# Cross-attention of a two-layer network: two transposes moved in TensorE's order, one small transfer moved to another queue

## The chip, the core and the metric

The kernel runs on one core of a Trainium2 chip. The metric is the device time of one execution in microseconds (us). Before the change three runs gave 2221.7, 2225.9 and 2228.41 us; the median is 2225.9 us.

TensorE (PE in the profile; PEld is its weight loads) does matrix products and transposes into PSUM, VectorE (DVE) and ScalarE (ACT) work on SBUF and PSUM, GpSimd (POOL) on SBUF, and SyncE (SP) issues most of the DMA transfers. Each engine has its own instruction stream and goes through it in order; the streams are tied together by semaphores.

## The reference

Two layers over 32 batches of 112 tokens with 512 features. The first attends to a context of 375 rows per batch and gates the result. The second does rotary self-attention with two sets of expert weights, then cross-attention over the same context, then a gated MLP with two sets of expert weights. The change lies in the cross-attention of the second layer:

```python
ci = rms_norm(hidden_states, ln_post_cross_w)
cq = heads(ci @ cq_w, NH, CHD)                 # 16 heads of 16
ckv = encoder_outputs @ ckv_w
ck, cv = jnp.split(ckv, 2, axis=-1)
cctx = sdpa(cq, ck, cv, causal=False)          # softmax(cq ck / sqrt(CHD)) cv
hidden_states = hidden_states + cctx.transpose(0, 2, 1, 3).reshape(b, l, CC) @ cdense_w
```

## The kernel before

The kernel runs in stages, each over all batches or token tiles: the first layer (names with `a_`), the projections of the second (`b_`), self-attention (`c_`), its output projection and the queries of the cross-attention (`d_`), the cross-attention (`e_`), and the MLP (`f_`). Products that need full precision are made of three: each operand is split into a high half (rounded to the fp32r type by ScalarE) and a low half (the rest, by VectorE or GpSimd), and `split_products` (lines 109 to 113) multiplies high by high, high by low and low by high.

The cross-attention is a software pipeline. There is one loop over steps `s` in each engine's function (`e_pe`, `e_dve`, `e_act`, `e_sp`, `e_pool`), and a step works on four batches at once: it prepares keys, queries and values of batch `s + 2`, takes the scores and their maxima of batch `s`, computes the scores once more by key with the maxima subtracted, and their exponentials, for batch `s - 1`, and finishes the context and its dense product for batch `s - 2`. The order inside a step is written out by hand for each engine.

TensorE's order in a steady step (`e_pe`, from line 1918): `scores(s, 0)`; `context(s - 2)`; `maximum_turn(s - 1)`, a transpose of the maxima into PSUM bank 7 (line 1890); `scores(s, 1)` (line 1848); `turn(s - 2)`, four transposes of the context (line 1895); `e_key_products(s + 2)`, twelve products into banks 4 and 5; `back(s - 2)`, two transposes of the normalised context (line 1901); `scores(s, 2)`; `queries_turn(s + 2)`, two transposes of the queries into banks 4 and 5 beside the keys (line 1815); `values(s + 2)`, eighteen products into banks 6 and 7; `scores(s, 3)`; `scores_by_key(s - 1, 0)` and `(s - 1, 1)` (line 1867); half of the dense product; and so on to the last groups by key. The scores use banks 0 to 2, and each group waits for the maximum of the group before it. `scores_by_key` writes banks 4 to 7, so its first group waits until the keys and queries of batch `s + 2` have been read from banks 4 and 5 (`e_kq_lo`), and for the transfer of the maxima (`e_max_placed`).

VectorE's order (`e_dve`, from line 2018): `maximum(s, 0)` (line 1970); `maximum_turned(s - 1)`, the copy of the turned maxima to SBUF (line 1987); `maximum(s, 1)`; `norm(s - 2)`, a reciprocal and a product (lines 2003 and 2005), which `back` waits for; `maximum(s, 2)`; `keys_queries_low(s + 2)` (line 1993); the copy of the last values; the low half of the context; the other maxima.

ScalarE's order (`e_act`, from line 1780): `raw(s - 2)`, the copy of the context out of PSUM (line 1769), which `turn` waits for; the high half of the memory (line 1366); the high half of the context, once `back` is done (line 1789); the high half of keys and queries, once the queries are turned (line 1403); values; the exponentials (line 1763); the copy of the dense product.

SyncE's order (`e_sp`, from line 1709): memory and query rows of later batches (lines 1653 and 1658); `place_maximum(s - 1)`, the transfer of the turned maxima, 14 KB, into two rows of the queries' tile (line 1690), which first waits for VectorE's copy; `place_both(s + 1)`, six transfers of keys and six of queries (lines 1675 and 1686); the stores of split keys and queries (line 1661). Behind the stage's loop SyncE loads the first rows of the MLP stage (lines 2079 and 2082), which VectorE adds up (line 2239) and ScalarE squares (line 2149).

Of the kernel before, what the change touches and what calls it, by code (L numbers as in the profile page):

```python
# [5 lines left out]
F32 = mybir.dt.float32  # L6
# [8 lines left out]
BATCHES, SEQ, DIM = 32, 112, 512  # L15
# [6 lines left out]
HEADS, HD = 16, 32  # L22
# [93 lines left out]
def build_xattn(nc, x_t, mem_t, mem_n, mem_e, weights, e_weights, q_weights, w_gate_mem, w_mem, b_gate,  # L116
# [3 lines left out]
    with ExitStack() as ctx:  # L120
# [1241 lines left out]
        def e_memory_high(act, b):  # L1362
            act.wait_ge(e_m_loaded[b % 2], 16 * (b // 2 + 1))
            if b >= 2:
                act.wait_ge(e_v, 2 * (b - 1))
            act.copy(e_m_parts[b % 2][0], e_m[b % 2]).then_inc(e_m_hi, 1)
# [242 lines left out]
        e_max_placed = Later(const_loaded, 16 * len(loads))  # L1609
# [9 lines left out]
        e_queries = [rv(at, (CT, PAIRS, SEQ)) for at in (4096, 5888, 19168)]  # L1619
        e_c_parts = both(20960, (CT, SEQ))  # L1620
        e_max_tok = [rv(25536 + 128 * i, (P,), SEQ) for i in range(2)]
        e_max_t = rv(25792, (SEQ,))
# [4 lines left out]
        def e_split(b):  # L1627

            return b + 2
# [20 lines left out]
        def e_sp(sp):  # L1650
            def load_memory(b):
                sp.wait_ge(e_m_lo, b - 1)
                sp.dma_start(e_m[b % 2], mem_e[b]).then_inc(e_m_loaded[b % 2], 16)

            def load_queries(b):
                if b >= 2:
                    sp.wait_ge(e_k, e_split(b - 2))
                sp.dma_start(e_cq[b % 2], cq_rows[b * SEQ:(b + 1) * SEQ]).then_inc(e_cq_loaded[b % 2], 16)

            def store(b, x, wide, into):  # L1660
                sp.dma_start(into[b, :, x].rearrange("t d (g s) -> (d g) t s", g=PAIRS), e_split_parts(b)[x][:, :, wide].bitcast(F32)).then_inc(
                    e_stored.sem, 16)

            def store_both(b):
                for x, made in enumerate((e_kq_hi, e_kq_lo)):
                    sp.wait_ge(made, e_split(b))
                    store(b, x, keys, k_rows)
                    store(b, x, queries, q_rows)

            def place_keys(b):  # L1670
                sp.wait_ge(*stored(b))
                into, done = e_keys[b % 3].rearrange("p g s -> p (g s)").bitcast(F32), e_placed[b % 2].sem
                for t in range(CT):
                    for part, x in enumerate((0, 1, 0)):
                        sp.dma_start(rows_of(into, t, part), k_rows[b, t, x]).then_inc(done, 16)

            def place_both(b):
                if b < 3:
                    sp.wait_ge(*e_cleared.at(1 if b == 1 else 3))
                else:  # L1680
                    sp.wait_ge(e_st, KEY_UNITS * (b - 2))
                place_keys(b)
                into, done = e_queries[b % 3].rearrange("p t g s -> p t (g s)").bitcast(F32), e_placed[b % 2].sem
                for t in range(CT):
                    for part, x in enumerate((0, 0, 1)):
                        sp.dma_start(rows_of(into, t, part)[:, t], q_rows[b, t, x]).then_inc(done, 16)

            def place_maximum(b):
                sp.wait_ge(e_mxt_made, b + 1)
                sp.dma_start(e_queries[b % 3][MAX_ROW:MAX_ROW + 2].bitcast(F32), e_max_t[0:2 * HEADS].bitcast(F32)).then_inc(  # L1690
                    e_max_placed.sem, 16)

            for b in (2, 3):
                load_memory(b)
            for x, made in enumerate((e_kq_hi, e_kq_lo)):
                sp.wait_ge(made, 1)
                store(0, x, keys, k_rows)
            place_keys(0)
            sp.wait_ge(*d_scattered.at(16 * BLOCKS))
            load_queries(0)  # L1700
            load_queries(1)
            sp.wait_ge(e_ones, 4 + 2 + 1)
            sp.wait_ge(e_kq_hi, 2)
            for part in (0, 1):
                place_queries(sp, part, e_kq_parts[0])
            load_queries(2)
            base = sp.value_load(base_f[0:1, 0:1], min_val=W_F, max_val=W_F + F_CHUNKS)
            store_both(1)
            for s in range(BATCHES + 1):
                if s + 4 < BATCHES:  # L1710
                    load_memory(s + 4)
                if s + 3 < BATCHES:
                    load_queries(s + 3)
                if s:
                    place_maximum(s - 1)
                if s + 1 < BATCHES:
                    place_both(s + 1)
                if s + 2 < BATCHES:
                    store_both(s + 2)
                if 2 <= s < 2 + RING:  # L1720
                    ring_load(sp, M_F + s - 2, chunk_at(base, s - 2))
# [30 lines left out]
        def e_act(act):  # L1752
            def values(b):
                act.wait_ge(e_v, 2 * b + 1)
                act.copy(e_cv[b % 4][:, 0:2, :, 0:CHD], ps[0:KC, e_key_bank(b) + 2, :].rearrange("p (c h d) -> p c h d", c=2, h=HEADS)).then_inc(
                    e_v_act, 1)

            def exponents(b, u):
                act.wait_ge(e_st, KEY_UNITS * b + u + 1)
                if b and u % NKC == 0:  # L1760
                    act.wait_ge(e_ctx, CT * (b - 1) + u // NKC + 1)
                at = 4 + 2 * (u % 2)
                act.activation(e_pt[:, u], ps[0:KC, at:at + 2, 0:4 * SEQ], ACT.Exp).then_inc(e_exp, 1)  # L1763

            def raw(b):
                act.wait_ge(e_ctx, 2 * b + 2)
                if b:
                    act.wait_ge(e_turned, b)
                act.copy(e_raw_t, ps[:, 3, 0:NT]).then_inc(e_raw, 1)

            e_memory_high(act, 2)
            values(0)
            values(1)
            act.wait_ge(e_k, 2)
            e_high(act, 0, queries)
            act.wait_ge(e_kq_lo, 2)
            place_queries(act, 2, e_kq_parts[1])
            act.wait_ge(e_k, e_split(1))
            e_high(act, 1, slice(0, CEVEN + SEQ))
            for s in range(BATCHES + 2):  # L1780
                if s == BATCHES + 1:
                    f_squares(act, 0)
                if s >= 2:
                    raw(s - 2)
                if s + 3 < BATCHES:
                    e_memory_high(act, s + 3)
                if s >= 2:
                    act.wait_ge(e_back, s - 1)
                    act.copy(e_c_parts[0], ps[:, 3, 0:CT * SEQ].rearrange("p (t s) -> p t s", t=CT)).then_inc(e_c_hi, 1)
                if s == BATCHES + 1:  # L1790
                    f_input_high(act, 0)
                if s + 2 < BATCHES:
                    act.wait_ge(e_k, e_split(s + 2))
                    e_high(act, s + 2, slice(0, CEVEN + SEQ))
                    values(s + 2)
                if 4 <= s < 4 + RING:
                    ring_high(act, M_F + s - 4)
                if 1 <= s <= BATCHES:
                    for u in range(KEY_UNITS - 2):
                        exponents(s - 1, u)  # L1800
                if s >= 2:
                    b = s - 2
                    act.wait_ge(e_cd, b + 1)
                    if b >= 2:
                        act.wait_ge(*e_scattered[b % 2].at(16 * (b // 2)))
                    act.copy(e_out[b % 2], ps[0:SEQ, 3, :]).then_inc(e_cd_out, 1)  # L1806
                if 1 <= s <= BATCHES:
                    for u in range(KEY_UNITS - 2, KEY_UNITS):
                        exponents(s - 1, u)

        def e_pe(pe):
# [106 lines left out]
            for s in range(BATCHES + 2):  # L1918
# [3 lines left out]
                if old:  # L1922
                    context(s - 2, 0)
                    context(s - 2, 1)
                if by_key:
                    maximum_turn(s - 1)
                if now:
                    scores(s, 1)
                if old:
                    turn(s - 2)  # L1930
                if new:
# [3 lines left out]
                if s == BATCHES + 1:  # L1935
                    f_turn(pe, 0, 0)
                    f_turn(pe, 0, 1)
                if now:
                    scores(s, 2)
                if new:  # L1940
                    queries_turn(s + 2)
                    values(s + 2, range(NKC))
                if now:
                    scores(s, 3)
# [19 lines left out]
        def e_dve(dve):  # L1964
# [53 lines left out]
            for s in range(BATCHES + 2):  # L2018
                if s < BATCHES:
                    maximum(s, 0)  # L2020
                if 1 <= s <= BATCHES:
                    maximum_turned(s - 1)
                if s < BATCHES:
                    maximum(s, 1)
                if s == BATCHES + 1:
                    f_add(dve, 0)
                    f_means(dve, 0)
# [419 lines left out]
```

## Time and profile before

| | |
|---|---|
| median of three runs | 2225.9 us |
| the profiled execution's own time | 2228.36 us |
| its span, first to last instruction | 2226.6 us |
| mean granted TensorE clock | 0.980 of full speed |
| TensorE busy | 95% of the span |
| VectorE, ScalarE, GpSimd busy | 57%, 47%, 40% |
| cross-attention stage | from about 1001 to 1517 us of the span, 32 steps |

A row of the timeline gives the start in us from the span's start, the length in us, the engine, the line of the kernel, the operation, output and inputs with their shapes, and how many like instructions in a row it merges. In brackets stands the engine's idle time ahead of it and what ended it. Matmuls overlap, so the distance between two starts says more than the length of one.

### The profile page before, as it was taken

Reading aid. Unit: us, or ns where it says so; the run is one execution under the profiler, and the core shown is the slowest. Engines: PE = TensorE matmul, PEld = TensorE weight load, DVE = VectorE, ACT = ScalarE, POOL = GpSimd, SP = SyncE. Lnnn points to the kernel's source line nnn. Section 1 sums busy time; section 2 is a strip of 40 time slices with the busy share of each in tenths; the row PEclk is TensorE's granted clock in tenths of the full one; section 3 lists DMA queues with packets and bytes.
Section 4 is the critical chain, followed back from the end, with each engine's and each line's share of the span. In section 5 each row is a group of like instructions: output and inputs, shape, how many; then the busy total and the mean of one; then the engine's idle time right before and its main releaser. Section 6 shows DMA issues by size and latency. Waiting matters only on the chain.

```text
span 2226.6 us, 40571 instructions
## 1 busy us (share of the span) xinstructions
PE 2117.5 (95%) x16042; PEld 1825.1 (82%) x16042; DVE 1276.0 (57%) x1910; ACT 1055.6 (47%) x1875; POOL 880.1 (40%) x741
## 2 busy tenths in 40 slices
PE   7999999999889889997999999988999999999998
PEld 6899998888667768887888888877888888888887
DVE  6755547756599984545666666654444344444343
ACT  5344335344278765443565555544334334344333
POOL 2211027676534324452111111104454554555456
PEclk9999999999999999997999999989999999999999
DMA  6343335665554446556777777645343443434333
GB/s 238 129 141 127 125 144 178 214 238 203 197 183 144 141 150 244 224 187 186 233 232 211 218 214 206 205 128 191 119 134 117 136 152 109 140 120 129 113 93 121
DMA packets 155613, 373.70 MB, mean 168 GB/s; under 512 B 40160, under 2 KB 60992, under 8 KB 145696
## 3 DMA queue, kind: packets, MB, share of 16 engines
q1 hardware_dynamic: 136416, 310.70, 44.1%
q0 software_dynamic: 18720, 60.29, 7.5%
q8 instruction: 128, 2.10, 0.4%
q14 instruction: 61, 0.50, 0.1%
q10 hardware_dynamic: 288, 0.11, 0.0%
HBM read 269.28 MB, written 100.93 MB: 166 GB/s over the span
## 4 chain that ended last, share of the span: by engine, by line
PE 82%; DVE 12%; DMA 3%; ACT 1%; issue 1%; SPq 0%; POOL 0%; POOLq 0%; DVEq 0%; ACTq 0%
PE ps L111 21%; PE ps L113 21%; PE ps L112 21%; PE ps L1848 5%; PE ps L1880 3%; PE ps L1867 3%; DVE f_arena L1311 2%; DVE c_max L1306 2%; PE ps L688 2%; DVE e_negmax L1970 2%; DVE c_sum L1317 1%; DMA f_arena<-qk_rows 1%; DVE r_arena L179 1%; DVE f_arena L1328 1%; PE ps L1895 1%
## 5 line engine op out<-in xcount | busy, mean ns | idle before, releaser
L111 PE MATMUL ps<-r_arena 128*128 128x512 f32 (+6 forms) x2410 | 894.0, 371 | 17.5 <-DVE r_arena L179 11.1
L112 PE MATMUL ps<-r_arena 128*128 128x512 f32 (+6 forms) x2410 | 882.9, 366 | 0.0
L113 PE MATMUL ps<-r_arena 128*128 128x512 f32 (+6 forms) x2410 | 882.9, 366 | 0.0
L179 POOL TENSOR_TENSOR r_arena<-f_arena,r_arena 128x512 fp32r<-128x512 f32 (+1 forms) x434 | 579.5, 1360 | 571.6 <-ACT r_arena L201 423.2
L111 PEld LDWEIGHTS ps<-r_arena 128*128 128x128 f32 (+2 forms) x2410 | 455.8, 189 | 81.7 <-POOL r_arena L179 11.0
L113 PEld LDWEIGHTS ps<-r_arena 128*128 128x128 f32 (+2 forms) x2410 | 455.3, 189 | 65.7
L112 PEld LDWEIGHTS ps<-r_arena 128*128 128x128 f32 (+2 forms) x2410 | 456.2, 189 | 60.2
L201 ACT CAST r_arena<-f_arena 128x512 fp32r<-128x512 f32 x400 | 235.8, 620 | 173.7 <-PE ps L113 128.1
L1970 DVE TENSOR_REDUCE e_negmax<-ps 112x3 f32<-112x1125 f32 (+1 forms) x192 | 230.0, 1198 | 135.8 <-PE ps L1848 135.6
L2277 DVE SCALAR_TENSOR_TENSOR f_arena<-f_arena,ps 128x512 f32<-128x512 f32 (+1 forms) x88 | 57.4, 652 | 231.2 <-ACT f_arena L2172 227.4
L1763 ACT ACTIVATE f_arena<-ps 125x896 f32<-125x896 f32 x192 | 165.3, 916 | 45.3 <-PE ps L1867 45.2
L2176 ACT CAST r_arena<-f_arena 128x512 fp32r<-128x512 f32 (+1 forms) x88 | 52.2, 593 | 246.9 <-DVE f_arena L2281 246.9
L179 DVE TENSOR_TENSOR r_arena<-f_arena,r_arena 128x512 fp32r<-128x512 f32 (+4 forms) x145 | 124.2, 873 | 75.9 <-ACT r_arena L2176 58.1
L1848 PE MATMUL ps<-r_arena 96*112 96x376 f32 x512 | 133.5, 364 | 21.1 <-DVE e_negmax L1970 17.0
L1726 POOL DMA_INDIRECT cd_rows<-f_arena,slot_all x32 | 30.0, 937 | 283.5 <-ACT f_arena L1806 283.5
L2281 DVE SCALAR_TENSOR_TENSOR f_arena<-f_arena,ps 128x512 f32<-128x512 f32 (+1 forms) x88 | 57.6, 654 | 104.1 <-PE ps L113 103.8
L2172 ACT ACTIVATE f_arena<-ps 128x512 f32<-128x512 f32 (+1 forms) x88 | 50.2, 571 | 139.0 <-PE ps L113 139.0
L1867 PEld LDWEIGHTS ps<-r_arena 98*125 98x125 f32 x768 | 101.3, 194 | 14.8 <-ACT f_arena L1763 10.4
L1867 PE MATMUL ps<-r_arena 98*125 98x224 f32 x768 | 111.8, 283 | 1.0 <-ACT f_arena L1763 0.6
L1848 PEld LDWEIGHTS ps<-r_arena 96*112 96x112 f32 x512 | 80.1, 186 | 38.8 <-DVE e_negmax L1970 20.8
L517 POOL TENSOR_TENSOR a_rstd<-a_ss,minus_half 112x2 f32<-112x2 f32 x16 | 11.3, 705 | 202.4 <-DVE a_ss L807 202.3
L1171 POOL TENSOR_TENSOR f_arena<-f_arena 112x448 f32<-112x448 f32 x32 | 36.4, 1137 | 136.6 <-ACT f_arena L1211 136.6
(213 smaller groups left out, 2564.1 us busy)
## 6 DMA issues: line engine op xcount, KB each, us to landing
f_arena<-weights SPq DMA_DIRECT2D x400, 256.0 KB, 2.9
r_arena<-k_rows SPq DMA_DIRECT2D x192, 188.0 KB, 3.5
k_rows<-r_arena SPq DMA_DIRECT2D x64, 376.0 KB, 3.0
f_arena<-rows SPq DMA_DIRECT2D x14, 1160.0 KB, 5.2
f_arena<-qk_rows SPq DMA_DIRECT2D x32, 448.0 KB, 4.1
f_arena<-mem_n SPq DMA_DIRECT2D x8, 1536.0 KB, 6.8
f_arena<-mem_e SPq DMA_DIRECT2D x32, 376.0 KB, 4.9
f_arena<-mem_t SPq DMA_DIRECT2D x16, 750.0 KB, 5.6
```

The costliest lines, as they stand in the source:

```text
L111: first = pe.matmul(out, w_hi, x_hi, start=start, stop=False)
L112: pe.matmul(out, w_hi, x_lo, start=False, stop=False)
L113: return first, pe.matmul(out, w_lo, x_hi, start=False, stop=stop)
L179: return engine.tensor_tensor(out, source, high.bitcast(F32), ALU.subtract)
L201: act.copy(w_hi[:, m % RING, :], w_raw[:, m % RING, :]).then_inc(w_hi_made, 1)
L1763: act.activation(e_pt[:, u], ps[0:KC, at:at + 2, 0:4 * SEQ], ACT.Exp).then_inc(e_exp, 1)
L1848: last = pe.matmul(ps[0:SEQ, h - s_heads[u][0], 0:CEVEN], e_queries[b % 3][0:MAX_ROW, h % 2, h // 2, :], e_keys[b % 3][0:MAX_ROW, h // 2, ...
L1867: last = pe.matmul(ps[0:KC, 4 + 2 * (u % 2) + n // 2, n % 2 * 2 * SEQ:(n % 2 + 1) * 2 * SEQ], e_keys[b % 3][0:MAX_ROW + 2, pair, m], e_que ...
L1880: last = pe.matmul(ps[32 * a:32 * a + 32, 3, batch(n)], e_cv[b % 4][:, c, 4 * n + a, :], e_pt[:, NKC * t + c, half, batch(a)], start=c == ...
L1970: dve.tensor_reduce(e_negmax[:, b % 2, heads[0]:heads[-1] + 1], ps[0:SEQ, 0:len(heads), 0:CTX], AX_X, ALU.max, negate=True).then_inc(e_max ...
L2277: dve.scalar_tensor_tensor(act_a[:, s, w], act_t[:, s, w], 1.0, ps[:, bank, w], ALU.add, ALU.mult).then_inc(f_acted, 1)
L2281: dve.scalar_tensor_tensor(act_h[:, s, w], act_a[:, s, w], 0.5, ps[:, bank + 1, w], ALU.mult, ALU.mult).then_inc(f_glu_made, 1)
```

## The change

Three things change, all of them in the cross-attention. On TensorE the turn of the maxima goes behind the second group of scores, next to the turn of the context; and the turn of the queries goes ahead of the third group of scores, next to the turn back. On VectorE the copy of the turned maxima goes behind the second maximum. And the transfer of the maxima is issued by ScalarE, between the high half of the memory and that of the context, instead of by SyncE.

```diff
@@ e_sp
-            def place_maximum(b):
-                sp.wait_ge(e_mxt_made, b + 1)
-                sp.dma_start(e_queries[b % 3][MAX_ROW:MAX_ROW + 2].bitcast(F32), e_max_t[0:2 * HEADS].bitcast(F32)).then_inc(
-                    e_max_placed.sem, 16)
-
...
                 if s + 3 < BATCHES:
                     load_queries(s + 3)
-                if s:
-                    place_maximum(s - 1)
                 if s + 1 < BATCHES:
                     place_both(s + 1)
@@ e_act
+            def place_maximum(b):
+                act.wait_ge(e_mxt_made, b + 1)
+                act.dma_start(e_queries[b % 3][MAX_ROW:MAX_ROW + 2].bitcast(F32), e_max_t[0:2 * HEADS].bitcast(F32)).then_inc(
+                    e_max_placed.sem, 16)
+
...
                 if s + 3 < BATCHES:
                     e_memory_high(act, s + 3)
+                if 1 <= s <= BATCHES:
+                    place_maximum(s - 1)
                 if s >= 2:
                     act.wait_ge(e_back, s - 1)
@@ e_pe
                 if old:
                     context(s - 2, 0)
                     context(s - 2, 1)
+                if now:
+                    scores(s, 1)
                 if by_key:
                     maximum_turn(s - 1)
-                if now:
-                    scores(s, 1)
                 if old:
                     turn(s - 2)
...
+                if new:
+                    queries_turn(s + 2)
                 if now:
                     scores(s, 2)
                 if new:
-                    queries_turn(s + 2)
                     values(s + 2, range(NKC))
@@ e_dve
                 if s < BATCHES:
                     maximum(s, 0)
+                    maximum(s, 1)
                 if 1 <= s <= BATCHES:
                     maximum_turned(s - 1)
-                if s < BATCHES:
-                    maximum(s, 1)
```

## Rows read from the trace of the kernel before

**Rows 1.** The page: busy us of each engine, share of the span, instructions.
```profile
PE 2117.5 (95%) x16042; PEld 1825.1 (82%) x16042; DVE 1276.0 (57%) x1910; ACT 1055.6 (47%) x1875; POOL 880.1 (40%) x741
```

**Rows 2.** Table by stretches: one steady step; length, busy us, granted clock, DMA.
```profile
1256.05:1271.36 15.31, 15.05 (x181) 13.33 (x181) 10.05 (x15) 8.81 (x13) 2.76 (x3) 1.00 0.70 209
```

**Rows 3.** Timeline of that step, TensorE's matmuls.
```profile
1259.19 0.32 PE L1890 MATMUL ps<-ident,r_arena 112*128 112x112 f32 x1
1259.27 0.75 PE L1848 MATMUL ps<-r_arena 96*112 96x376 f32 x3
1259.91 0.65 PE L1895 MATMUL ps<-ident,f_arena 128*112 128x128 f32 x4
...
1262.44 0.35 PE L1901 MATMUL ps<-ident,f_arena 112*128 112x112 f32 x2
1262.57 0.75 PE L1848 MATMUL ps<-r_arena 96*112 96x376 f32 x3
1263.15 0.36 PE L1815 MATMUL ps<-ident,f_arena 112*128 112x112 f32 x2
...
1265.47 0.68 PE L1848 MATMUL ps<-r_arena 96*112 96x376 f32 x3
1265.99 1.03 PE L1867 MATMUL ps<-r_arena 98*125 98x224 f32 x8
1266.86 0.39 PE L111 MATMUL ps<-r_arena 128*112 128x512 f32 x1
```

**Rows 4.** Timeline of that step, TensorE's weight loads.
```profile
1259.91 0.40 PEld L1895 LDWEIGHTS ps<-ident,f_arena 128*112 128x112 f32 x4 [0.22 <-ACT f_arena L1769]
...
1265.83 1.00 PEld L1867 LDWEIGHTS ps<-r_arena 98*125 98x125 f32 x8
```

**Rows 5.** Timeline of that step, VectorE.
```profile
1259.54 0.28 DVE L1987 CAST r_arena<-ps 128x112 fp32r<-128x112 f32 x1 [1.35 <-PE ps L1890]
1260.06 1.33 DVE L1970 TENSOR_REDUCE e_negmax<-ps 112x3 f32<-112x1125 f32 x1 [0.24 <-PE ps L1848]
1261.30 0.25 DVE L2003 RECIPROCAL e_rsum<-ps 112x16 f32<-112x16 f32 x1
1261.59 0.42 DVE L2005 TENSOR_TENSOR f_arena<-ps,e_rsum 112x256 f32<-112x256 f32 x1
1263.35 1.33 DVE L1970 TENSOR_REDUCE e_negmax<-ps 112x3 f32<-112x1125 f32 x1 [1.34 <-PE ps L1848]
1264.60 1.16 DVE L1993 SCALAR_TENSOR_TENSOR r_arena<-ps,r_arena 128x976 fp32r<-128x976 f32 x1
```

**Rows 6.** Timeline of that step, ScalarE.
```profile
1262.83 0.35 ACT L1789 CAST r_arena<-ps 128x224 fp32r<-128x224 f32 x1 [2.26 <-PE ps L1901]
1263.55 0.99 ACT L1403 ACTIVATE r_arena<-ps 128x976 fp32r<-128x976 f32 x1 [0.37 <-PE ps L1815]
```

**Rows 7.** SyncE: timeline of that step; its waits over the span (us, times, longest).
```profile
1259.84 0.69 SPq L1690 DMA_DIRECT2D r_arena<-r_arena  x1
...
SPq L1690 <- DVE r_arena L1987: 110.6, 32, 15.3
```

**Rows 8.** Timeline of an early step, TensorE, 1050.6 to 1052.3 us.
```profile
1050.67 0.68 PE L1848 MATMUL ps<-r_arena 96*112 96x376 f32 x3
1051.19 0.95 PEld L1867 LDWEIGHTS ps<-r_arena 98*125 98x125 f32 x8 [0.17 <-issue]
...
1052.16 0.40 PE L111 MATMUL ps<-r_arena 128*112 128x512 f32 x1
```

**Rows 9.** Timeline of the stage's end.
```profile
1476.37 0.42 DVE L2005 TENSOR_TENSOR f_arena<-ps,e_rsum 112x256 f32<-112x256 f32 x1
...
1476.85 0.41 PE L1901 MATMUL ps<-ident,f_arena 112*128 112x112 f32 x2 [1.50 <-DVE f_arena L2005]
...
1516.28 0.63 ACT L2149 ACTIVATE f_arena<-f_arena 128x512 f32<-128x512 f32 x1 [0.52 <-DVE f_arena L2239]
```

**Rows 10.** DMA issues, 1100 to 1460 us: KB each, median us to landing.
```profile
f_arena<-cq_rows SPq DMA_DIRECT2D x23, 112.0 KB, 4.7
```

## The prediction

> **What bounds the kernel now.** I read the page first: TensorE is busy for 2117.5 us, 95% of the span [rows 1]. A change that leaves TensorE's work as it is can therefore gain only where TensorE stands idle, and costs time wherever it makes TensorE wait. Next I read the table by stretches over one steady step of the cross-attention (32 batches, one step each): 15.31 us, TensorE busy for 15.05 of them at a granted clock of 1.00 (the 2.4 GHz level) [rows 2]. ScalarE (8.81 us) and VectorE (10.05 us) have room as sums; what matters is where they stand in TensorE's order.
>
> Then the timeline of that step. TensorE goes through the turn of the maxima at 1259.19, the second group of scores at 1259.27, the turn back at 1262.44, the third group at 1262.57, the turn of the queries at 1263.15, the value products, the fourth group at 1265.47 and the first group by key at 1265.99 [rows 3]. The reader should see that none of these rows has a wait in brackets. Two waits are nearly there, though. The load of the turn of the context starts 0.22 us late, released by ScalarE's copy of that context [rows 4]. And the scores by key write over the PSUM banks from which VectorE still takes the low halves of keys and queries (line 1993). That subtraction ends at 1264.60 + 1.16 = 1265.76 [rows 5], and the weight load of the first group by key starts at 1265.83 [rows 4], the engines' hand-over later. TensorE is through with the fourth group of scores at about 1265.99, so this wait costs nothing today, and has nothing to spare.
>
> **The change, part by part.**
>
> *Turn of the maxima behind the second group of scores.* The same transpose, moved. Before, it takes 1259.27 - 1259.19 = 0.08 us ahead of the scores [rows 3]; afterwards it stands between the scores and the turn of the context. That turn waits for ScalarE's copy either way, which depends on the context alone, and the copy released the load at 1259.91 [rows 4]. So the second group may start some 0.06 to 0.08 us earlier, but the turn of the context, and all behind it, does not: 0 us. From below: if an alternation of transposes and products costs something by itself, there is a gain, priced as a rival.
>
> *VectorE: the copy of the turned maxima behind the second reduction.* The copy (0.28 us) stood in idle time [rows 5]. Now it stands between the reduction and the normalising of the previous batch, for which the turn back waits. The reduction starts 0.06 us earlier, at 1260.00; the next operation followed 1.24 us behind it; with the copy's 0.28 to 0.30 us the reciprocal moves from 1261.30 to about 1261.53, and the product ends at 1261.59 + 0.42 + 0.23 = 1262.24 [rows 5]. In a later step, where the turn back did wait for it, the transpose began 1476.85 - 1476.37 - 0.42 = 0.06 us behind the product [rows 9]. So the turn back could start at 1262.30 and is due at 1262.44 [rows 3]: covered, with 0.14 us left; with that cover gone each 0.1 us costs 3 us over the stage. In the last two steps with scores (no key products) the cover is gone: 0.23 us each, **+0.4 us**.
>
> *Turn of the queries next to the turn back.* This is the dear part. The two transposes of the queries are like the two of the turn back, which take 1262.57 - 1262.44 = 0.13 us to the next start, and the first product behind them is stretched: three matmuls of the third group take 1263.15 - 1262.57 = 0.58 us, those of the fourth 1265.99 - 1265.47 = 0.52 us [rows 3]. Together 0.19 us, by which the third group of scores comes later. The value products and the fourth group are as late as before in TensorE's own order, since the same transposes have only changed sides. But VectorE takes the third maximum (from 1263.35) and right behind it, with no gap, the low halves (1264.60) [rows 5]. Both move 0.19 us; the first load by key moves from 1265.83 to 1266.02, while TensorE is ready for it when it was. ScalarE's high halves (1263.55 + 0.99 = 1264.54, [rows 6]) come some 0.4 us earlier, but in VectorE's order the maximum goes first, so nothing uses that.
>
> What does a late load cost? An early step shows it: there the same load was 0.17 us late, and from the fourth group of scores to the next dense product went 1052.16 - 1050.67 = 1.49 us [rows 8], against 1266.86 - 1265.47 = 1.39 us [rows 3]: 0.10 us. A load 0.19 us late then costs 0.12 to 0.13 us; the bounds are 0 (all hidden) and 0.20 us (nothing hidden), and I take 0.13, as the row is near. It falls in the 29 steps that have both scores by key and a batch to prepare: **+3.8 us** (0 to 5.8). Behind it everything of the step moves together, the exponentials and the next scores too, so it is not won back. The first step, paced by the maxima: **+0.2 us**.
>
> *The transfer of the maxima from ScalarE.* SyncE issued it at 1259.84 for 0.69 us, and in all waited 110.6 us there [rows 7]; its 12 placements of keys and queries a step were queued behind that wait. They go earlier now, but no step of the steady stretch ends its idle time on them: 0 us gained. On ScalarE the wait sits between the high half of the memory and the high half of the context. VectorE's copy would end at about 1261.52; with the issue's 0.69 us ScalarE is free at 1262.25, and its next work, released by the turn back, starts at 1262.83 [rows 6]: hidden, 0.6 us left; with that cover gone the high half of the context comes late, and behind it that of keys and queries, which has only its 0.4 us to give. The transfer itself leaves 1.7 us later than before and is needed at 1265.83, 4.3 us after its issue.
>
> *The end of the stage.* SyncE no longer waits for the last maxima before it loads the first rows of the last stage, so these land earlier. ScalarE waited 0.52 us for the sum made from them [rows 9] and is then held by its own exponentials, so at most that is won: **-0.5 us**.
>
> **Sum:** 3.8 + 0.2 + 0.4 - 0.5 = 3.9 us, and 0.1 us for the step in which the turn of the maxima no longer lies in a wait: **+4.0 us**. The rows come from the profiled execution, whose own time of 2228.4 us lies 2.5 us above the median of the three runs, 2225.9; both move alike, so 2232.4 for that execution, and **2229.9 us** for the median, 0.18% slower. What a measurement of this kernel can tell from no change is about 0.3%, 6.7 us.
>
> **Rivals.**
>
> *Fewer alternations pay (faster).* If products run slower behind a transpose for the alternation's sake, grouping wins it back. Most that rows allow: the second group takes 1259.91 - 1259.27 = 0.64 us and the third 0.58 against 0.52 [rows 3], so 0.12 + 0.06 = 0.18 us, in 30 steps 5.4 us, and 0.5 at the end: 2220 us. Against it: 0.06 of the 0.12 us is the wait for the copy [rows 4], and the turn back and the turn of the queries follow products without any gap. It holds only if the low halves do not come late as well. Chance 0.10.
>
> *The low halves are not late after all (no change).* If VectorE's subtraction was held by ScalarE's high half, which ended 0.06 us before it started (1264.54 and 1264.60), and not by the maximum, it would not follow the maximum by the whole 0.19 us. Then 2226 us. Against it: the maximum's 1.25 us from start to the next start is VectorE's own pace (1.24 behind the second reduction, [rows 5]), so both held it. Chance 0.12.
>
> *The maxima land too late (slower).* The first group by key waits for the transfer too. If it takes as long from issue to landing as the queries' rows, 4.7 us in this stretch [rows 10], against the 4.3 us that it has, the load waits 0.4 us, of which 0.13 is in the sum already; with 5.1 us it would be 0.8 us. Over 31 steps 10 to 20 us: 2240 to 2250 us. It decides from a landing later than 4.3 us. For it: SyncE's placements are now under way when it leaves. Against it: it is 14 KB. The page "DMA: Bandwidth & Descriptors" of the Trainium skill (Queues, rings and completion order) says that each DMA engine goes round-robin, packet by packet, between the queues that have work; by that rule the transfer waits behind a packet of SyncE's and not behind its backlog, and the landing stays in time. No transfer of this stage in the trace was issued by ScalarE, so nothing here shows it yet. Chance 0.08.
>
> **Numbers.** The forecast has 0.70, the rivals 0.10, 0.12 and 0.08. Faster by over 0.3% (below 2219.2) is about half of the first rival and some luck, 0.06. Slower by over 0.3% (above 2232.6) is the last rival, and of the forecast the part in which the load hides nothing (5.8 for 3.8) and the turn back waits as well: 0.20. Within it: 0.74. The range of 2221 to 2236.5 us takes in the bounds of the late load, the first rival's end nearly, and a turn back 0.1 us late.
>
> **What would show it.** In the steady step: the first load by key with a wait of about 0.2 us that VectorE's line of the low halves ended; a step of about 15.45 us; the turn of the context still released by ScalarE's copy; ScalarE's high half of keys and queries right behind that of the context; SyncE placing keys some 2 us earlier; no wait on the maxima's transfer. Wrong if the step stays at 15.31 us or falls, or if a wait on the transfer, or on the normalising before the turn back, stands there.

## The result, and the profile after

The changed kernel takes **2235.5 us** (median of 20 runs, 2230.0 to 2242.8), the kernel before in the same comparison 2229.2 us (20 runs): a ratio of **1.0034**, 95% interval 1.0026 to 1.0043, some 7.6 us slower (5.8 to 9.6; the two medians are 6.3 us apart). I had forecast 0.18%, and no difference that can be measured as the likeliest case. The profiled execution took 2233.25 us, its span is 2231.4 us.

The page of the changed kernel: first the busy times, then one line of its DMA queues (packets, MB, share of 16 engines).

```profile
PE 2120.0 (95%) x16042; PEld 1825.2 (82%) x16042; DVE 1272.3 (57%) x1910; ACT 1053.4 (47%) x1875; POOL 880.5 (39%) x741
...
q10 hardware_dynamic: 1376, 0.57, 0.1%
```

The work is the same as in [rows 1]. The queue on which ScalarE issues has 1376 packets, and had 288 before: the transfer of the maxima did change queues.

The table by stretches, one steady step of the changed kernel:

```profile
1251.85:1267.33 15.48, 15.23 (x181) 13.43 (x181) 9.95 (x15) 8.71 (x13) 2.75 (x3) 1.00 0.74 212
```

15.48 us against the 15.31 of [rows 2], at the same granted clock. One step is a sample; over the 27 steps between the first maxima of step 3 and of step 30 the mean is 15.47 us against 15.34, so **+0.13 us a step**. The timeline of this step, TensorE's matmuls:

```profile
1251.88 0.73 PE L1848 MATMUL ps<-r_arena 96*112 96x376 f32 x3 [0.25 <-DVE e_negmax L1971]
...
1254.98 0.77 PE L1848 MATMUL ps<-r_arena 96*112 96x376 f32 x3
1255.60 0.26 PE L1890 MATMUL ps<-ident,r_arena 112*128 112x112 f32 x1
1255.71 0.65 PE L1895 MATMUL ps<-ident,f_arena 128*112 128x128 f32 x4
...
1258.27 0.36 PE L1901 MATMUL ps<-ident,f_arena 112*128 112x112 f32 x2
1258.46 0.35 PE L1815 MATMUL ps<-ident,f_arena 112*128 112x112 f32 x2
1258.58 0.75 PE L1848 MATMUL ps<-r_arena 96*112 96x376 f32 x3
...
1261.30 0.69 PE L1848 MATMUL ps<-r_arena 96*112 96x376 f32 x3
1261.88 1.10 PE L1867 MATMUL ps<-r_arena 98*125 98x224 f32 x8
1262.82 0.39 PE L111 MATMUL ps<-r_arena 128*112 128x512 f32 x1
```

Read it against [rows 3] from the start of each step's first scores, which is 1251.88 here and 1256.08 before. The turn back stands at 6.39 us (before 6.36), the third group of scores at 6.70 (6.49), the fourth at 9.42 (9.39), the first dense product at 10.94 (10.78). So the third group comes 0.21 us later, the fourth hardly, and between the fourth group and the dense product 0.13 us are lost: 1.52 us against 1.39. That is nearly the whole of the step's loss, and it stands where the first group by key is. The weight loads of the same step:

```profile
1255.70 0.41 PEld L1895 LDWEIGHTS ps<-ident,f_arena 128*112 128x112 f32 x4
...
1261.85 0.95 PEld L1867 LDWEIGHTS ps<-r_arena 98*125 98x125 f32 x8 [0.20 <-issue]
```

The wait of the turn of the context for ScalarE [rows 4] is gone, and the load of the first group by key has a new one of 0.20 us. The profile calls what released it "issue"; VectorE's timeline and then ScalarE's, of the same step, say more:

```profile
1255.79 1.33 DVE L1971 TENSOR_REDUCE e_negmax<-ps 112x3 f32<-112x1125 f32 x1 [1.81 <-PE ps L1848]
1257.04 0.27 DVE L1988 CAST r_arena<-ps 128x112 fp32r<-128x112 f32 x1
1257.22 0.25 DVE L2004 RECIPROCAL e_rsum<-ps 112x16 f32<-112x16 f32 x1
1257.50 0.42 DVE L2006 TENSOR_TENSOR f_arena<-ps,e_rsum 112x256 f32<-112x256 f32 x1
1259.37 1.33 DVE L1971 TENSOR_REDUCE e_negmax<-ps 112x3 f32<-112x1125 f32 x1 [1.44 <-PE ps L1848]
1260.62 1.17 DVE L1994 SCALAR_TENSOR_TENSOR r_arena<-ps,r_arena 128x976 fp32r<-128x976 f32 x1
```

```profile
1257.34 0.62 ACTq L1760 DMA_DIRECT2D r_arena<-r_arena  x1
...
1258.66 0.35 ACT L1789 CAST r_arena<-ps 128x224 fp32r<-128x224 f32 x1 [2.29 <-PE ps L1901]
1258.90 0.99 ACT L1403 ACTIVATE r_arena<-ps 128x976 fp32r<-128x976 f32 x1
```

The low halves end at 1260.62 + 1.17 = 1261.79 and the load starts at 1261.85, 0.06 us behind them (0.07 before). ScalarE's high halves end at 1258.90 + 0.99 = 1259.89, 0.73 us before VectorE begins the low halves: they no longer hold anything. ScalarE is through with its issue at 1257.96, 0.70 us ahead of its next work.

The stage's end looks quite different. Behind the last step with scores comes a step that has only the scores by key of the last batch and what follows them; the last transfer of the maxima is needed there. The timeline of SyncE, ScalarE and TensorE in this step of the changed kernel:

```profile
1504.80 0.34 SPq L2082 DMA_DIRECT2D f_arena<-cd_rows  x1
...
1505.27 0.62 ACTq L1760 DMA_DIRECT2D r_arena<-r_arena  x1
...
1510.30 2.02 PE L1867 MATMUL ps<-r_arena 98*125 98x224 f32 x8 [3.11 <-DMA r_arena<-r_arena]
1512.12 0.63 PE L111 MATMUL ps<-r_arena 128*112 128x512 f32 x1
```

And the same place before, first SyncE's own order:

```profile
1507.29 0.66 SPq L1690 DMA_DIRECT2D r_arena<-r_arena  x1
1507.99 0.41 SPq L2079 DMA_DIRECT2D f_arena<-h_rows  x1
1508.51 0.36 SPq L2082 DMA_DIRECT2D f_arena<-cd_rows  x1
```

and then the table of waits at that place, TensorE (us, times, longest):

```profile
PE ps L1867 <- DMA r_arena<-r_arena: 0.3, 1, 0.3
```

Before, SyncE issued the maxima and only then the first rows of the MLP stage. Now the load of those rows, 1 MB, is issued 0.47 us ahead of the maxima, and TensorE waits 3.11 us for 14 KB. In the trace's records of DMA packets the load's 128 packets of 8 KB run from 1505.78 to 1509.45 us, and the 32 packets of ScalarE's queue from 1509.36 to 1509.80: 4.1 us from issue to the first packet, where the steady steps show 1.3 to 2.3. Behind the wait TensorE is slow as well. The table by stretches, after, from the first dense product on; and then 1512 to 1525 us of the span before, where the first dense product starts at 1510.46:

```profile
1512.00:1527.90 15.90, 12.32 (x140) 10.58 (x140) 4.19 (x11) 10.09 (x20) 4.97 (x5) 0.71 0.29 94
```

```profile
1512.00:1525.00 13.00, 8.76 (x130) 7.48 (x131) 5.98 (x13) 8.42 (x17) 4.59 (x5) 0.88 0.56 206
```

The granted clock is 0.71 behind the wait and was 0.88 there. The two stretches differ in length and place; over the 16 us from the first dense product on it is 0.71 after and 0.89 before, and 0.79 in a second trace of the kernel before, so part of this varies by itself. The first dense products take 0.63 us, at the lower level (1.2 GHz), where the steady step has 0.39, and those at this place before have 0.40. From the first maximum of the last step with scores to the first tanh of the MLP stage go 47.7 us; before it was 41.6.

So the time is lost in two places: a tenth of a microsecond in each steady step, and some microseconds once, in the step behind the last scores.

### The profile page after: what moved, and what is told of

Same layout as the page of the kernel before. It is cut to its first block, busy times and chain, and to the rows that moved or that the text cites. A ratio compares the mean times of both kernels' runs of the same rounds, so it can differ in the third digit from the quotient of the medians.

```text
span 2231.4 us, 40571 instructions
## 1 busy us (share of the span) xinstructions
PE 2120.0 (95%) x16042; PEld 1825.2 (82%) x16042; DVE 1272.3 (57%) x1910; ACT 1053.4 (47%) x1875; POOL 880.5 (39%) x741
## 3 DMA queue, kind: packets, MB, share of 16 engines
q10 hardware_dynamic: 1376, 0.57, 0.1%
## 4 chain that ended last, share of the span: by engine, by line
PE 82%; DVE 10%; DMA 4%; ACT 1%; issue 1%; SPq 1%; POOL 0%; POOLq 0%; DVEq 0%; ACTq 0%
PE ps L111 21%; PE ps L113 21%; PE ps L112 21%; PE ps L1848 5%; PE ps L1880 3%; PE ps L1867 3%; DVE f_arena L1311 2%; DVE c_max L1306 2%; PE ps L688 2%; DVE e_negmax L1971 2%; DMA f_arena<-qk_rows 2%; DVE r_arena L179 1%; DVE c_sum L1317 1%; PE ps L2189 1%; PE ps L1895 1%
## 5 line engine op out<-in xcount | busy, mean ns | idle before, releaser
L2172 ACT ACTIVATE f_arena<-ps 128x512 f32<-128x512 f32 (+1 forms) x88 | 50.3, 571 | 139.1 <-PE ps L113 139.1
L1848 PEld LDWEIGHTS ps<-r_arena 96*112 96x112 f32 x512 | 78.0, 181 | 43.9 <-DVE e_negmax L1971 20.3
```

The source lines that it names most:

```text
L1848: last = pe.matmul(ps[0:SEQ, h - s_heads[u][0], 0:CEVEN], e_queries[b % 3][0:MAX_ROW, h % 2, h // 2, :], e_keys[b % 3][0:MAX_ROW, h // 2, ...
```

## The experiments

The two theories I tested. *Lateness*: in the steady step the turn of the queries is dear because the third scores, VectorE's third maximum and its low halves come later by the turn's own length, not because transposes stand next to each other or next to products. *The queue*: at the end the maxima wait behind the 1 MB load, and what had kept them from it was SyncE's old wait. The rivals are named in the expectations.

All readings in one table: the mean steady step; TensorE's wait ahead of the last batch's first group by key ("end wait"); the time from the first maximum of the last step with scores to the first tanh of the MLP stage ("last step on"); and the ratio to the kernel before with its 95% interval, where there is more than the one profiled execution.

| kernel | step | end wait | last step on | ratio |
|---|---|---|---|---|
| before | 15.34 | 0.27 | 41.6 | |
| before again | 15.35 | 0.27 | 42.4 | |
| changed | 15.47 | 3.11 | 47.7 | 1.0034 (1.0026 to 1.0043) |
| changed, load behind the maxima | 15.46 | 0.24 | 41.1 | 1.0015 (1.0006 to 1.0024) |
| changed, queries' turn back | 15.35 | 2.99 | 47.7 | 1.0009 (1.0000 to 1.0019) |
| changed, both | 15.35 | 0.24 | 41.4 | 1.0000 (0.9989 to 1.0010) |
| before + queries' turn | 15.46 | 0.26 | 42.9 | 1.0020 (1.0011 to 1.0029) |
| before + issue from ScalarE | 15.36 | 2.84 | 45.5 | 1.0015 (1.0004 to 1.0026) |
| before + maxima's turn | 15.87 | 0.26 | 43.2 | 1.0103 (1.0087 to 1.0118) |
| changed, load in halves | 15.46 | 1.45 | 43.9 | 1.0030 (1.0018 to 1.0042) |
| before + values first | 16.01 | 0.28 | 43.3 | 1.0090 (1.0066 to 1.0114) |
| before + one transpose | 15.37 | 0.27 | 42.5 | |

**The load behind the maxima.** SyncE waits for the last transfer of the maxima before it loads the first rows of the MLP stage.

```diff
@@ e_sp, behind the loop, ahead of load_cross(0)
+            sp.wait_ge(*e_max_placed.at(MAX_PLACES * BATCHES))
```

> The changed kernel; only SyncE's load of the first cross-attention rows for the MLP stage now waits until the last transfer of the maxima has landed. Theory (queue): at the stage's end the transfer issued by ScalarE lay behind SyncE's 1 MB load in the DMA engines; then the 3.1 us wait of the last first group by key falls to 0.5 us or less, the clock there stays up, and the time falls about 6 us against the change: ratio to before about 1.000 to 1.002. Rival (ScalarE's queue is slow after a pause): the wait stays near 3 us and the ratio near 1.0034. The step stays at 15.47 us under both.

The timeline of the same step of this kernel:

```profile
1506.14 0.62 ACTq L1760 DMA_DIRECT2D r_arena<-r_arena  x1
1508.31 1.13 PE L1867 MATMUL ps<-r_arena 98*125 98x224 f32 x8 [0.24 <-DMA r_arena<-r_arena]
1508.35 0.34 SPq L2082 DMA_DIRECT2D f_arena<-cd_rows  x1
```

With no load ahead of it, the same transfer from the same queue is there 2.2 us after its issue, not 5.0 (1505.27 to 1510.30). ScalarE's queue is not slow; the load was in the way. The wait is back at 0.24 us, the time from the last step on at 41.1 us, and the ratio falls from 1.0034 to 1.0015, by 4.2 us. In the traces the end shrinks by 6.6 us; the timed runs give less.

**The queries' turn back in its place.** The changed kernel with `queries_turn` behind the third scores again.

```diff
-                if new:
-                    queries_turn(s + 2)
                 if now:
                     scores(s, 2)
                 if new:
+                    queries_turn(s + 2)
                     values(s + 2, range(NKC))
```

> The changed kernel with the turn of the queries back behind the third group of scores. Theory (late low halves): the step falls from 15.47 to 15.31 to 15.34 us, the first load by key has no wait, time 3.9 us below the change; the wait at the stage's end stays 3 us: ratio to before 1.001 to 1.002. Rival (the copy of the maxima in VectorE's order makes the turn back late): the step stays at 15.47 us and the ratio at 1.0034.

The step is 15.35 us, as before the change. The table of waits (us, times, longest) over 1100 to 1460 us shows what went with it. In the changed kernel:

```profile
PEld ps L1867 <- ACT f_arena L1756: 7.5, 23, 0.3
...
PEld ps L1867 <- issue: 4.4, 22, 0.2
PEld ps L1895 <- ACT f_arena L1767: 0.2, 1, 0.2
```

With the queries' turn back in its place:

```profile
PEld ps L1867 <- ACT f_arena L1756: 7.4, 23, 0.3
...
PEld ps L1895 <- ACT f_arena L1767: 0.2, 1, 0.2
```

The line with 22 waits of 0.20 us ahead of the first group by key goes with the queries' turn. The wait of the turn of the context, which in this stretch before the change was

```profile
PEld ps L1895 <- ACT f_arena L1769: 5.2, 24, 0.2
```

is all but gone in both, and the step is no shorter for it: the move of the maxima's turn buys nothing.

**The queries' turn alone.** The kernel before with only `queries_turn` moved, the edit above the other way round.

> The kernel before with only the turn of the queries moved next to the turn back. Theory (late low halves): the step is 15.47 us, 29 steps of 0.13 us, 3.9 us in all, ratio 1.0015 to 1.002; nothing changes at the stage's end. Rival (the copy of the maxima): step 15.34 us, ratio 1.000.

The step is 15.46 us and the ratio 1.0020: the loss per step comes with this part alone.

**Both mends in the changed kernel.** The two edits above together, so that of the change the maxima's turn, VectorE's later copy and the issue from ScalarE are left.

> The changed kernel with both mends: the turn of the queries back, and the load of the MLP's first rows behind the last transfer of the maxima. Theory: what is left is the turn of the maxima behind the second group of scores, the copy in VectorE's order and the issue by ScalarE, which cost nothing: step 15.31 to 15.34 us, ratio 0.999 to 1.0005; the two steps without key products keep 0.23 us each. Rival (something else of the change costs): ratio of 1.001 or more.

1.0000 (0.9989 to 1.0010): nothing is left of the loss, and there is no gain.

**The issue from ScalarE alone.** The kernel before with only `place_maximum` moved from `e_sp` to `e_act`.

> The kernel before with only the transfer of the maxima issued by ScalarE. Theory (queue): the step stays at 15.31 to 15.35 us, and at the stage's end the last first group by key waits about 3 us for the transfer, behind SyncE's 1 MB load; ratio 1.001 to 1.003. Rival (the transfer from ScalarE costs in every step): step above 15.4 us.

The step stays at 15.36 us and the last batch's first group by key waits:

```profile
1507.33 2.02 PE L1867 MATMUL ps<-r_arena 98*125 98x224 f32 x8 [2.84 <-DMA r_arena<-r_arena]
```

The ratio is 1.0015. The wait is nearly that of the changed kernel, but from the last step on it is 45.5 us and not 47.7. In the 16 us from the first dense product on the granted clock is 0.84 here and 0.71 there. That fits the difference of 2.2 us, but no run varies the clock alone.

**The maxima's turn alone.** The kernel before with `maximum_turn` behind the second scores and VectorE's copy behind the second maximum, the transfer still issued by SyncE.

```diff
@@ e_pe
+                if now:
+                    scores(s, 1)
                 if by_key:
                     maximum_turn(s - 1)
-                if now:
-                    scores(s, 1)
@@ e_dve
                     maximum(s, 0)
+                    maximum(s, 1)
                 if 1 <= s <= BATCHES:
                     maximum_turned(s - 1)
-                if s < BATCHES:
-                    maximum(s, 1)
```

> The kernel before with only the turn of the maxima behind the second group of scores and VectorE's copy behind the second maximum; SyncE still issues the transfer. Theory: 0.0 us a step (15.31 to 15.35), the turn of the context no longer waits for ScalarE's copy but starts as late, 0.2 us more in each of the two steps without key products; ratio 0.9995 to 1.0007. Rival (the normalising comes late for the turn back): step 15.4 us or more, with a wait on the product at line 2005.

This was a miss: 1.0103, the slowest kernel of all. Its timeline, TensorE's first scores of two steps and SyncE's issues:

```profile
1241.99 0.77 PE L1848 MATMUL ps<-r_arena 96*112 96x376 f32 x3 [1.63 <-DMA r_arena<-q_rows]
...
1257.67 0.77 PE L1848 MATMUL ps<-r_arena 96*112 96x376 f32 x3 [0.59 <-DMA r_arena<-q_rows]
...
1263.16 0.69 SPq L1690 DMA_DIRECT2D r_arena<-r_arena  x1
1263.97 3.68 SPq L1675 DMA_DIRECT2D r_arena<-k_rows  x6
```

And the line of its table of waits over 1100 to 1460 us (us, times, longest):

```profile
PE ps L1848 <- DMA r_arena<-q_rows: 17.0, 21, 1.6
```

SyncE's issue waits for the copy, which is later now: it goes out 5.49 us into the step (1263.16 - 1257.67), before 3.76 (1259.84 of [rows 7], less 1256.08). The twelve placements of keys and queries are queued behind it, 1.7 us later than before, and the next step's first scores wait for them, 21 times and 17.0 us in this stretch. The kernel with both mends has the same turn and the same copy, with ScalarE issuing, and no such wait. So the parts hang together: the later copy is free only because the issue left SyncE.

**The load in halves.** The changed kernel with the 1 MB load issued as two of 512 KB, of which the second waits for the last transfer of the maxima. If the maxima wait behind whatever was issued first, half the load should leave half the wait.

```diff
@@ e_sp, behind the loop
-            load_cross(0)
+            for half in (slice(0, TB // 2), slice(TB // 2, TB)):
+                if half.start:
+                    sp.wait_ge(*e_max_placed.at(MAX_PLACES * BATCHES))
+                sp.dma_start(f_cross(0)[:, half, :], tile_of(cd_rows, 0)[:, half, :]).then_inc(f_cd_loaded.sem, 16)
@@ f_add
-            dve.wait_ge(*f_cd_loaded.at(16 * (tile + 1)))
+            dve.wait_ge(*f_cd_loaded.at(16 * (tile + 2)))
```

> The changed kernel; SyncE's load of the first cross-attention rows is cut into two halves of 512 KB, and the second waits for the last transfer of the maxima. Theory (the transfer waits for all the bytes that SyncE has put ahead of it): in the changed kernel 1 MB took 3.7 us from its first packet to its last; half of that ahead leaves a wait of 1.0 to 1.6 us in place of 3.1. Rival (turn by turn between the queues): the wait is gone already, under 0.5 us, or unchanged near 3 us if ScalarE's queue is slow by itself. Step 15.47 us under all.

```profile
1504.73 0.62 ACTq L1760 DMA_DIRECT2D r_arena<-r_arena  x1
1508.10 1.87 PE L1867 MATMUL ps<-r_arena 98*125 98x224 f32 x8 [1.45 <-DMA r_arena<-r_arena]
...
1511.92 2.50 DVE L2242 TENSOR_TENSOR f_arena<-f_arena 128x512 f32<-128x512 f32 x4 [4.46 <-DMA f_arena<-cd_rows]
```

TensorE's wait is 1.45 us instead of 3.11: it goes with the bytes ahead of the transfer. In the records of packets the maxima's first one runs at 1506.84, 2.1 us after the issue, while packets of the load's first half still run until 1507.58. So the transfer does not wait until the last byte of what was issued ahead has moved; it may wait for the share of those DMA engines that it uses itself, which the records do not name. The time does not tell the two kernels apart (1.0030 against 1.0034). VectorE, in the lower row, waits 4.46 us for the second half; whether that gives the gain back was not tried.

**The kernel before again.** A second trace of the unchanged kernel, to see what varies by itself.

> The kernel before, profiled once more, to see what of the trace varies by itself: steady step 15.31 to 15.35 us, from the last step's first maximum to the first tanh of the MLP stage 41 to 43 us; the first three steps, 50.3 us in the first trace, may come out at 47 us as in four of the other five traces, since no part of the change reaches them the same way in all.

The steady step (15.35) and the end wait (0.27) repeat. The first three steps do not: 47.1 us in sum here, 50.3 in the first trace, and between 46.7 and 51.0 in all kernels, whichever edit they have. The changed kernel's trace happens to have 47.6 there. That is why the two spans differ by only 4.8 us: from the last step's first maximum to the end they differ by 7.1 (745.4 against 738.3), the 27 steady steps by 3.4 and the step behind them by 0.2, but the changed kernel's trace is 2.7 us shorter in the first three steps and 3.2 shorter ahead of the stage.

**The values first.** To tell lateness from the transposes: the kernel before with no transpose moved, and six of the value products ahead of the third scores.

```diff
+                if new:
+                    values(s + 2, (0,))
                 if now:
                     scores(s, 2)
                 if new:
                     queries_turn(s + 2)
-                    values(s + 2, range(NKC))
+                    values(s + 2, (1, 2))
```

> The kernel before with the first six of the eighteen value products ahead of the third group of scores; no transpose is moved. Theory (what is put between the turn back and the third group of scores makes the low halves late by its length): six products at 0.117 us are 0.70 us, of which about 0.06 is hidden as in the early step, so the step grows from 15.33 to 15.95 to 16.0 us, 29 times, ratio 1.008 to 1.009. Rival (it is the transposes standing side by side that cost): step 15.33 us, ratio 1.000.

The timeline of one step, VectorE and TensorE's load and group by key:

```profile
1237.50 1.16 DVE L1995 SCALAR_TENSOR_TENSOR r_arena<-ps,r_arena 128x976 fp32r<-128x976 f32 x1
...
1238.74 0.95 PEld L1867 LDWEIGHTS ps<-r_arena 98*125 98x125 f32 x8 [0.66 <-issue]
1238.77 1.10 PE L1867 MATMUL ps<-r_arena 98*125 98x224 f32 x8 [0.36 <-issue]
```

The low halves end at 1238.66, the load starts 0.08 us behind, 0.66 us late, and the step is 16.01 us. No transpose has moved, and the same wait is there, only larger. It is lateness.

**One transpose.** The other way, a smaller dose: the kernel before with one of the two queries' transposes ahead of the third scores.

> The kernel before with only one of the two transposes of the queries ahead of the third group of scores. Theory (lateness, with the first 0.06 us hidden): 0.10 us late, so the step grows by 0.03 to 0.06 us to 15.37 to 15.41 us, and the first load by key has a gap of about 0.1 us. Rival (transposes side by side cost): by half of 0.13 us or more, with no gap at the load by key.

The step is 15.37 us. The load by key is on average 0.09 us late (0.10 forecast). With nothing, one transpose, two, or six products ahead of the third scores the step is 15.34, 15.37, 15.46 and 16.01 us: the first transpose is nearly hidden, and what comes on top is paid.

## Why the prediction was wrong

Slower was right, the size was not: 0.34% against 0.18%. That the measured 2235.5 us lie inside the forecast range of 2221 to 2236.5 is luck: I had widened it for a load by key that hides nothing and for a late turn back, and neither came; what filled it stood in no step of the sum. By its own steps:

- *The turn of the maxima, 0 us.* Right in price. One sign that I had named failed: the turn of the context no longer shows a wait for ScalarE's copy, yet it starts 3.83 us into the step, as before. The turn back stands 6.39 us into the step, 6.36 before, and with only this, the copy and the issue left the ratio is 1.0000 (0.9989 to 1.0010). The rival by which fewer alternations pay falls with it: two groups of transposes were joined and no time came back.
- *VectorE's copy, covered.* Right, and with more cover than I gave it: the copy costs 0.18 us to the next start (1257.04 to 1257.22), not 0.28. I had not seen what its lateness would have done without the third part: with the issue left on SyncE it costs 1.0%. The +0.4 us of the two last steps with scores can't be told from what those steps vary by themselves.
- *The queries' turn, +3.8 us.* Right in mechanism and size. The third scores come 0.21 us later (0.19 forecast), the load is 0.20 us late (0.19), and that costs 0.13 us a step (0.12 to 0.13). Over 29 steps 3.8 us; in the timed runs the part alone costs 4.4 us (1.0020), taking it out of the changed kernel saves 5.6, and it leaves 3.3 where the end is mended. The rival by which the low halves are not late falls.
- *The first step, +0.2 us.* Not to be told: the first three steps vary by some 4 us in sum, with or without the change.
- *The transfer from ScalarE, 0 us in the steady steps.* Right: no wait on it there, and ScalarE had 0.70 us left (0.6 forecast). SyncE begins to place keys at 1251.66, 0.2 us ahead of the step's first scores, where before it was 4.6 us behind them (1260.65): 4.8 us earlier and not 2.
- *The end of the stage, -0.5 us.* **This step failed.** I saw that SyncE would load the first rows of the MLP stage earlier, and asked only who would have them sooner. I did not ask what this 1 MB would now stand ahead of. In its place stands a wait of 2.8 to 3.1 us, and behind it a granted clock of 0.71 in two of three kernels: 3 to 6 us in the traces, 2.0 to 4.2 us by the ratios (the changed kernel against the one with the load behind the maxima, and the same pair with the queries' turn back). Each ratio is uncertain by about 2 us, so the smaller of the two differences does not stand by itself; the issue from ScalarE alone costs 3.3 us (1.0015).

With 3.8 us for the steps and 2.0 to 4.2 for the end the two parts make 5.8 to 8.0 us; measured were 7.6 (5.8 to 9.6). The mechanism of the end was my third rival, maxima that land too late. I had placed it in every step, behind SyncE's placements of 56 and 188 KB, where it does not occur; it occurs once, behind a single large load. What the runs show at this place is a first packet 4.1 us after the issue, as the load's last ones ended. I had weighed the rival down with the round-robin between queues of which the page "DMA: Bandwidth & Descriptors" of the Trainium skill speaks (Queues, rings and completion order). By that page of the Trainium skill a DMA engine drains a whole packet of one queue before it turns to the next, and a packet is typically some 9 to 17 descriptors. The trace does not contradict this: it has 128 records of 8 KB and 16 of 4 bytes on SyncE's queue here, nine for each of the 16 DMA engines if they are shared out evenly, and if a record is one descriptor that is no more than one such packet. Whether they were one packet no run shows. What failed is my step from the rule to "not behind its backlog": I did not ask how much of a large load one packet can be.

What stays open is where the small transfer waits, since the traces show issue and packets and nothing between; how much of the end is the wait and how much the clock behind it; and how large the end is exactly, as its two pairs differ by a factor of two.

## What to carry to other kernels

A wait that looks idle can be what keeps a small urgent transfer ahead of a large one: when you take an issue out of a queue, follow the queue to the next large transfer, also past the end of the loop, and ask what that now overtakes. When an operation moves, look for every engine that waits on its result, in the order of that engine's queue: here the same late copy cost 1.0% or nothing, by who issued the transfer behind it. And a wait that nearly stands in the trace is a budget: work put ahead of it is hidden as far as the slack goes and is paid for beyond.

## What the runs showed of the hardware that was not expected

- A transfer of 14 KB on one engine's queue, issued 0.47 us after one of 1 MB on another engine's, had its first packet only as the large one ended, 4.1 us after its issue (1.3 to 2.3 us in the steady steps, behind placements of 56 and 188 KB); behind half of the load the wait ahead of TensorE was 1.45 us, not 3.11, and with the load held back 0.24.
- Behind a wait of 1.45 to 3.11 us TensorE was at the lower level (dense products of 0.63 us) in all four kernels that had one; at the same place it was at the higher level in the kernels without. Over the 16 us from there on the granted clock was 0.71 in two of the four and 0.83 and 0.84 in the others, and from 0.79 to 0.89 without the wait.
- Removing idle time of the weight loads is not removing time. The turn of the context's load lost a wait of 0.22 us in each step, and the step was no shorter, while a load 0.20 us late ahead of the group by key cost 0.13 us, and one 0.66 us late cost 0.67.
